# Value products of an attention core issued for two key blocks at a time, with 16 exponential tiles in place of 8

## The reference

```
def _L1_attn_ref(x, Wq, Wk, Wv):
...
        q = (x @ Wq.T).reshape(B, S, H, Hd)
        k = (x @ Wk.T).reshape(B, S, H, Hd)
        v = (x @ Wv.T).reshape(B, S, H, Hd)
        energy = jnp.einsum('bqhd,bkhd->bhqk', q, k)
        attn = jax.nn.softmax(energy / jnp.sqrt(jnp.float32(D)), axis=-1)
        out = jnp.einsum('bhqk,bkhd->bqhd', attn, v).reshape(B, S, D)
        return out
```

## Time and profile before

| | |
|---|---|
| median of 3 runs | 3273.67 us (3268.23 to 3277.1) |
| the profiled execution, its own time | 3280.04 us |
| its span in the profile | 3277.9 us |
| busy in the span: PE, DVE, ACT, POOL | 77%, 61%, 46%, 17% |
| mean granted clock of TensorE | 0.874 of full |
| the core that is changed | from about 716 to 1417 us of the span |

### The profile page before, as it was taken

The page is one execution under the profiler, slowest core; times in us unless marked ns, Lnnn a source line. Parts: engine busy times, 40 slices in busy tenths (PEclk is TensorE's granted clock), DMA queues, the critical chain, the costliest instruction groups (busy, mean ns, idle before and its releaser), DMA issues. The chain is left out here.

```text
span 3277.9 us, 45624 instructions
## 1 busy us (share of the span) xinstructions
PE 2517.5 (77%) x16417; PEld 1220.7 (37%) x16417; DVE 1984.8 (61%) x3063; ACT 1518.9 (46%) x3040; POOL 549.0 (17%) x843
## 2 busy tenths in 40 slices
PE   2998523459999999957995799999677886766478
PEld 1776222312222222125674233333245545534423
DVE  2553477678888888531114677776285384458655
ACT  1232212217778777733432366666356356432211
POOL 3000011000000000000001111111174174104045
PEclk8998657659999999978997699999689998977689
DMA  2111000111111111002001000000110010000000
GB/s 69 47 50 40 1 9 0 44 56 39 38 37 39 43 43 43 3 17 52 1 1 38 29 23 26 26 26 11 46 34 5 1 30 2 1 6 2 1 20 13
DMA packets 57227, 82.88 MB, mean 25 GB/s; under 512 B 23114, under 2 KB 35564, under 8 KB 56620
## 3 DMA queue, kind: packets, MB, share of 16 engines
q1 hardware_dynamic: 57004, 79.97, 7.8%
HBM read 65.32 MB, written 14.02 MB: 24 GB/s over the span
## 5 line engine op out<-in xcount | busy, mean ns | idle before, releaser
L849 DVE TENSOR_REDUCE l1a_core_mpart<-l1a_core_psA 128x1 f32<-128x1024 f32 x512 | 601.5, 1220 | 96.8 <-PE l1a_core_psA L769 96.8
L831 ACT ACTIVATE l1a_core_prob<-l1a_core_psB 128x512 f32<-128x512 f32 x1024 | 552.1, 595 | 206.0 <-PE l1a_core_psB L780 204.4
L1159 ACT ACTIVATE l2a_core_prob<-l2a_core_psB 128x384 f32<-128x384 f32 (+3 forms) x656 | 316.0, 525 | 196.7 <-PE l2a_core_psB L1101 191.9
L1181 DVE TENSOR_REDUCE l2a_core_mpart<-l2a_core_psA 128x1 f32<-128x1024 f32 (+7 forms) x384 | 335.5, 909 | 118.0 <-PE l2a_core_psA L1088 68.0
L780 PE MATMUL l1a_core_psB<-l1a_core_qh,l1a_core_kh 75*128 75x512 bf16 x1024 | 312.0, 387 | 4.7 <-ACT l1a_core_prob L831 4.7
L791 PE MATMUL l1a_core_psV<-l1a_core_prob,l1a_core_vh 128*32 128x512 f32 x2048 | 274.4, 608 | 7.0 <-ACT l1a_core_oh L823 6.9
L769 PE MATMUL l1a_core_psA<-l1a_core_ka,l1a_core_qa 64*128 64x512 bf16 x1024 | 173.2, 403 | 67.9 <-DVE l1a_core_mpart L849 36.4
L1084 PE MATMUL l2a_core_psA<-l2a_core_kh,l2a_core_qh 72*128 72x512 bf16 (+3 forms) x640 | 181.3, 367 | 36.7 <-DMA l2a_core_kh<-kparts 31.3
L1101 PE MATMUL l2a_core_psB<-l2a_core_qh,l2a_core_kh 75*128 75x384 bf16 (+3 forms) x688 | 206.9, 349 | 2.8 <-DMA l2a_core_qh<-l2a_core_mT 2.6
L1117 PE MATMUL l2a_core_psV<-l2a_core_prob,l2a_core_vh 128*32 128x128 f32 (+3 forms) x1856 | 195.2, 444 | 15.0 <-ACT l2a_core_prob L1159 9.4
L1860 DVE SCALAR_TENSOR_TENSOR X<-l1e_psO,W,X 128x128 f32<-128x128 f32 x128 | 36.0, 344 | 220.6 <-PE l1e_psO L1817 220.6
(11 more groups left out here) (632 smaller groups left out, 4444.4 us busy)
## 6 DMA issues: line engine op xcount, KB each, us to landing
l1a_core_qa<-qparts SPq DMA_DIRECT2D x64, 96.0 KB
l1a_core_ka<-kparts SPq DMA_DIRECT2D x32, 192.0 KB
l0a_core_kh<-kparts SPq DMA_DIRECT2D x48, 96.0 KB
l0a_core_qh<-qparts SPq DMA_DIRECT2D x48, 96.0 KB
l1a_core_qh<-qparts SPq DMA_DIRECT2D x48, 96.0 KB
l1a_core_kh<-kparts SPq DMA_DIRECT2D x16, 288.0 KB
l2a_core_qh<-qparts SPq DMA_DIRECT2D x48, 96.0 KB
l2a_core_kh<-kparts SPq DMA_DIRECT2D x16, 288.0 KB
```

Source lines behind the costliest of these rows:

```text
L831: nc.scalar.activation(prob[u % (2 * PER_KB)][:], psB[u % 3][:], ACT.Exp, scale=scale).then_inc(b_exped, 1)
L849: nc.vector.tensor_reduce(mpart[:, n // 2, n % 2:n % 2 + 1], psA[i % 2][:], AX.X, ALU.max).then_inc(a_freed, 1)
L1159: nc.scalar.activation(prob[n % RING][:, 0:cols], psB[n % 3][:, 0:cols], ACT.Exp, scale=scale).then_inc(b_exped, 1)
L1181: ins = nc.vector.tensor_reduce(mpart[:, place, part:part + 1], psA[i % 2][:, lo * P:hi * P], AX.X, ALU.max)
```

## The change

`values` is called for two key blocks, one after the other, at every even key block (kb - 2 and kb - 1), in place of once at every key block (kb - 1). The last two key blocks of the last head follow at the end. The ring `prob` has 16 tiles in place of 8, and an exponential waits for the `values` call of four key blocks before in place of two. The tile sizes, the slots, their order and the number of instructions are as before.

```diff
--- before.py
+++ after.py
@@ -609,11 +609,11 @@
 
 
     st = Stage(nc, name)
-    NU, PER_KB, LEAD, GAP = 2 * NT, NC, 8, 4
+    NU, PER_KB, LEAD, GAP, RING = 2 * NT, NC, 8, 4, 4 * NC
     qa, ka = [[st.sb(f"{n}{i}", [P, S], BF16) for i in range(2)] for n in ("qa", "ka")]
     qh, kh = [[st.sb(f"{n}{i}", [P, S], BF16) for i in range(3)] for n in ("qh", "kh")]
     vh = [st.sb(f"vh{i}", [P, NT, 32]) for i in range(2)]
-    prob = [st.sb(f"prob{i}", [P, CH]) for i in range(2 * PER_KB)]
+    prob = [st.sb(f"prob{i}", [P, CH]) for i in range(RING)]
     oh = [st.sb(f"oh{i}", [P, CH]) for i in range(2)]
     mpart = st.sb("mpart", [P, NT, 2])
     negm = [st.sb(f"negm{i}", [P, NT]) for i in range(2)]
@@ -788,7 +788,7 @@
                     if h:
                         pe.wait_ge(o_copied, h)
                 for c in range(NC):
-                    ins = mm(psV[32 * c:32 * c + 32, :], vh[h % 2][:, kb, :], prob[(u + c) % (2 * PER_KB)][:],
+                    ins = mm(psV[32 * c:32 * c + 32, :], vh[h % 2][:, kb, :], prob[(u + c) % RING][:],
                              start=kb == 0, stop=kb == NT - 1, skip_group_check=True)
                 ins.then_inc(pv_done, 1)
 
@@ -807,11 +807,11 @@
                         done += 1
                     score(h, kb, 2)
                     score(h, kb, 3)
-                    if kb:
-                        values(h, kb - 1)
-                    elif h:
-                        values(h - 1, NT - 1)
-            values(H - 1, NT - 1)
+                    if kb % 2 == 0 and h + kb:
+                        for e in (2, 1):
+                            values(*divmod(NT * h + kb - e, NT))
+            for kb in (NT - 2, NT - 1):
+                values(H - 1, kb)
 
         @block.scalar
         def _(act):
@@ -826,9 +826,9 @@
                 for n in range(PER_HEAD):
                     u = PER_HEAD * h + n
                     act.wait_ge(b_scored, u + 1)
-                    if u >= 2 * PER_KB:
-                        act.wait_ge(pv_done, u // PER_KB - 1)
-                    nc.scalar.activation(prob[u % (2 * PER_KB)][:], psB[u % 3][:], ACT.Exp, scale=scale).then_inc(b_exped, 1)
+                    if u >= RING:
+                        act.wait_ge(pv_done, u // PER_KB - 3)
+                    nc.scalar.activation(prob[u % RING][:], psB[u % 3][:], ACT.Exp, scale=scale).then_inc(b_exped, 1)
                     if n == 5 and h:
                         copy_o(h - 1)
             copy_o(H - 1)
```

## The result

The changed kernel takes 3396.95 us (median of 4 runs, 3392.21 to 3408.86) against 3272.43 (median of 4) for the kernel before, 124.5 us more. A second timing gave 1.0395 (1.0350 to 1.0441). The forecast was 3385 us, within a range of 3355 to 3425.

The account below looks back on a forecast made before the run. PE, 97% busy, was taken to bind by a hair over DVE. Rounds +94.6, head ends +8.0, copies -7.8, last head +4.2 made +99; with +12 for the clock, 3273.7 became 3385 us, range 3355 to 3425.

Parts of the forecast that it names:

- The round: Two key blocks with A: 6.15 us in place of 5.24, 0.91 more, 104 times, 94.6 us in all.
- The timetable: Computed starts on PE, DVE and ACT through a round of two: PE waits 0.37 for ACT and 0.69 for DVE.
- The rival that the switches decide: PE alone sets the pace, both waits gone: 29 us saved, 3244 us; chance 0.05.
- the rival of ACT's wait alone: psA comes free earlier, so only the wait for ACT is paid: round 5.46, +19 us, 3293; chance 0.04.
- V behind V: Value products directly behind value products on PE: the first call takes 0.91 us; other bound 1.00, 0.09 more.
- What it gives back: Head's first value products no longer wait for the copy of psV: 0.52 us less a head, 15 times, -7.8.
- the price: The psV copy's cost on ACT in the odd key block, hidden by the wait for DVE; otherwise 0.5 us a head.
- the clock term: PE clock falls behind clustered waits at head ends: +12 us, between nothing and 14 x 1.12 = 16.
- falls at most head ends and none elsewhere: Where PE's clock drops: at most head ends, where waits of 1.27, 0.41 and 0.34 us come within 3.6.
- rounds without A: Last head: eight S then two V end at 5.27 us against 4.80, 0.47 more, 9 times, +4.2.
- the round with the transpose: Key block 12 of head 14: wait of 1.78 us for POOL stays, end at 7.5 against 6.60, 0.9 more.
- The first case: DVE's wait as in the step-by-step schedule sets the time; chance 0.82, own range 3365 to 3405 us.

Follow-up runs that it names:

- half_max_pair: Changed kernel with each DVE maximum reading only the first 512 of its 1024 scores; 1.0000 times the kernel before, 44.51 us a head.
- changed_again: The changed kernel's file, unaltered, timed a second time against the kernel before; ratio 1.0395, 51.17 us a head.
- light_third_pair: Changed kernel with a head's third A slot moved from its last key block to the one before, which holds the transpose; 1.0281 times the kernel before.
- pair_last_only: Kernel before with the ring of 16 and value products in pairs in the last head alone; 1.0028 times the kernel before, tail 55.7 us.
- pair_but_last: Changed kernel with one value call a key block again in the last head only; 1.0339 times the kernel before, tail 55.7 us.
- light_third_early_copy: Kernel before with the third A slot moved to the transpose's key block and the psV copy two exponentials earlier; 0.9894 times the kernel before.

## Why the prediction was right

*The round.* The timetable held to 0.02 us at each of its steps up to V, and the round to 0.06. The mechanism is shown by taking it away: without the wait for DVE the round is 5.40, without that for ACT as well 5.02, and what the change takes away, two switches of PE, is then a gain. The rival that the switches decide is what happens with more buffers; with these it fell. So did the rival of ACT's wait alone, which is half_max_pair's state.

*V behind V.* I took 0.91 for the first of two calls. Two calls take 1.85 where one takes 1.00, so the pair costs 0.85 more than one: from the second on, passes come 0.43 apart, not 0.455. This is the 0.05 or 0.06 by which the round is shorter than forecast. The weight loads of the third and of the fourth pass are recorded one pass ahead of them (1004.42 + 0.45 + 0.43 = 1005.30 is the start of the third pass):

```profile
1004.87 0.13 PEld L791 LDWEIGHTS l1a_core_psV<-l1a_core_prob,l1a_core_vh 128*32 128x32 f32 x4 [0.30 <-issue]
1005.30 0.13 PEld L791 LDWEIGHTS l1a_core_psV<-l1a_core_prob,l1a_core_vh 128*32 128x32 f32 x4 [0.30 <-issue]
```

The Trainium skill's case of the background weight buffer ("TensorE: Matmul & The Clock Gate") agrees with this. The Trainium skill's statement on the same page that loads overlap only where the row group differs does not hold for these products, which all use the same rows; here the measurement decides.

*What it gives back.* The wait for the copy is gone. The copy now delays ACT, and through it the fourth S of a row:

```profile
1029.54 0.39 PE L780 MATMUL l1a_core_psB<-l1a_core_qh,l1a_core_kh 75*128 75x512 bf16 x1 [0.59 <-ACT l1a_core_prob L831]
1029.86 0.90 PE L769 MATMUL l1a_core_psA<-l1a_core_ka,l1a_core_qa 64*128 64x512 bf16 x4
1030.69 0.60 PE L780 MATMUL l1a_core_psB<-l1a_core_qh,l1a_core_kh 75*128 75x512 bf16 x2
```

PE waits 0.59 there in place of 0.20, and then 0.4 less for DVE (A to S 0.83 in place of 1.23). The round is 6.09 as all others: the price is hidden as forecast.

*The clock, head ends.* Falls at head ends and none in ordinary rounds with A: right. A head costs 7.29 more, where the timetable gives 6.42 and the clock term 12/14 = 0.86, together 7.28. That agreement is two small errors that cancel: the seven ordinary rounds are 0.38 shorter in all than forecast, and the head end is 8.52 where the timetable without a fall gives 7.29 less 0.05, so a fall costs 1.28 and comes in every head of this execution. changed_again shows the same price directly (heads of 49.9 without a fall, 51.2 with one), and that the waits do not bring a fall every time: three heads of thirteen had none. light_third_pair takes the falls away, but for one.

*The clock, last head.* This is the term that was mis-sized. The prediction says "falls at most head ends and none elsewhere", and for the stretch behind the last transpose it has 4.2 for rounds without A and 0.9 for the round with the transpose, about 5. Measured are 19.4: rounds of two take 6.83 in place of the forecast 5.27, with the clock at half for half of the time. The timetable's part was right here too, since the same round without a fall takes 5.21 in pair_last_only. pair_but_last gives 14 of it back. These 14 us are nearly the whole difference between the 111 forecast and the 126 that the core lost: in the thirteen equal heads stand 94.7 (forecast 94.6), in heads 0 and 14 together 12.1 (11.3), in the tail 19.4 (5.1). Why the clock falls every time there and only twice in pair_last_only stays open; the rounds are the same in both, and only what ran before differs.

*The range.* The first case's own upper bound was given as 3405, but its terms (3273.7 + 99 + 10 + 16) add up to 3399. The measured 3397 lies below both.

## What to carry to other kernels

Joining two bursts on an in-order engine saves its switches, but spreads everything else unevenly: before joining, compare the new distances between refills with what the buffers hold. Here two psA buffers carry DVE for 2.3 us (two maxima 1.14 apart), and from the last A of one pair to DVE's start on the next pair it is now 3.7 (1003.56 to 1007.24). Where an order already leaves one engine 0.26 us of slack in 2.62, look instead for single waits at the seams (third slot and copy), which gave 1% here. And where the clock can fall, a wait costs more than its length.

## What was not expected of the hardware

After one wait of 1.8 us the clock stayed at half for 3.4 us in the kernel before and for 23.9 in light_third_early_copy, though PE ran the same four S and V behind it without an idle microsecond (15.00 busy of 15.00 in the row above). It does not always rise again as soon as PE is busy.

The Trainium skill's advice on gaps between matmuls ("TensorE: Matmul & The Clock Gate", "Why this matters for your kernels") speaks of single gaps; no idle gap of PE at a head end of the changed kernel is longer than 1.11 us in the profile, and the clock fell there in each of 14 heads in one execution and in most heads of another. Several short waits close together can do what that section of the Trainium skill ascribes to one long one.

A stage whose instructions nobody touched differed by 12 us between the two profiled executions, by its clock alone. A difference of 0.3% in the whole time of this kernel is therefore better read from the stage that was changed.
